# Row part of the position bias: one product for both heads of a pair; the residual read in the middle of the attention

## The reference, cut to what matters

```python
x = x + _L0_conv_ref(_gn(x), ...)     # neighbourhood attention, 7 x 7, 16 registers
x = x + _L1_conv_ref(_gn(x), ...)     # full attention with a position bias
```

```python
q = q * scale
attn = jnp.einsum('bqd,bkd->bqk', q, k)
rel_h = jnp.einsum('bhwc,hkc->bhwk', r_q, Rh)      # row part: depends on the query and the key's row
rel_w = jnp.einsum('bhwc,wkc->bhwk', r_q, Rw)      # column part
attn = attn + rel_h[..., :, None] + rel_w[..., None, :]
out = softmax(attn) @ v, then proj_w, proj_b
```

## Time and profile before

| | us |
|---|---|
| median of the runs | 3226.82 |
| profiled execution, its own time | 3222.15 |
| its span, first to last instruction | 3220.3 |
| TensorE busy | 2905.4 (90%) |
| VectorE busy | 2476.7 (77%) |
| GpSimd busy | 1902.8 (59%) |
| ScalarE busy | 1861.9 (58%) |
| `front` of layer 2 | about 868 to 1218 |
| `attention_full` | 1218 to about 3112 |

### The profile page before, as it was taken

One profiled execution on the slowest core, in us unless ns is written; L12 is line 12 of the kernel. 1 busy time (PEld: TensorE's weight loads), 2 busy tenths in 40 slices (PEclk: granted clock), 3 DMA queues, 4 the chain that ended last, 5 costly groups with the idle time before them and its releaser, 6 DMA issues. The chain is left out here.

```text
span 3220.3 us, 82906 instructions
## 1 busy us (share of the span) xinstructions
PE 2905.4 (90%) x34200; PEld 1874.4 (58%) x34200; DVE 2476.7 (77%) x5171; ACT 1861.9 (58%) x3434; POOL 1902.8 (59%) x1561
## 2 busy tenths in 40 slices
PE   4996999997579885999999999999999999999977
PEld 2453677774335442666666666666666666666644
DVE  6754888885666534888888888888888888888854
ACT  3333676664344432666666666666666666666655
POOL 3452555552110123777777777777777777777762
PEclk9896999998789986999999999999999999999989
DMA  3326555555437658322222222222222233332115
GB/s 142 155 89 147 135 135 141 142 140 192 143 108 215 195 131 203 63 51 52 51 52 52 51 51 51 51 52 52 51 51 51 52 61 59 58 59 54 21 42 147
DMA packets 219836, 301.91 MB, mean 94 GB/s; under 512 B 134394, under 2 KB 172884, under 8 KB 213972
## 3 DMA queue, kind: packets, MB, share of 16 engines
q1 hardware_dynamic: 219460, 296.62, 37.7%
HBM read 196.56 MB, written 92.64 MB: 90 GB/s over the span
## 5 line engine op out<-in xcount | busy, mean ns | idle before, releaser
L1746 POOL TENSOR_TENSOR fprob_low<-fprob 128x768 f16<-128x768 f32 x1008 | 1449.2, 1468 | 445.2 <-ACT fprob L1714 445.2
L1757 DVE TENSOR_REDUCE fpart_max<-fmax_acc 128x1 f32<-128x384 f32 x2592 | 1354.0, 556 | 252.0 <-PE fmax_acc L1585 235.9
L1714 ACT ACTIVATE fprob<-fscores 128x768 f32<-128x768 f32 x1296 | 1049.3, 810 | 592.5 <-PE fscores L1614 592.4
L1585 PE MATMUL fmax_acc<-fk_m,fq_m 128*128 128x384 f16 x2592 | 847.8, 327 | 32.6 <-DMA fident<-in_ident 27.6
L1612 PE MATMUL fscores<-fq_a,fk_a 128*128 128x384 f16 x2592 | 843.0, 325 | 10.6 <-DMA fk_m<-in_one_m 10.6
L1614 PE MATMUL fscores<-fq_b,fk_b 97*128 97x384 f16 x2592 | 846.9, 327 | 0.0
L1638 PE MATMUL fout_acc<-fv,fprob 128*128 128x65 f16 x7776 | 609.4, 191 | 2.5 <-POOL fprob_low L1746 2.1
L1639 PE MATMUL fout_acc<-fv,fprob_low 128*128 128x33 f16 x7776 | 593.8, 179 | 0.0
L1638 PEld LDWEIGHTS fout_acc<-fv,fprob 128*128 128x128 bf16 x7776 | 541.6, 97 | 76.5 <-POOL fprob_low L1746 5.2
L1639 PEld LDWEIGHTS fout_acc<-fv,fprob_low 128*128 128x128 f16 x7776 | 485.6, 96 | 72.5
L1131 POOL TENSOR_TENSOR prob_low<-prob 128x242 f16<-128x242 f32 (+2 forms) x360 | 250.0, 717 | 254.7 <-ACT prob L1089 252.9
(11 more groups left out here) (134 smaller groups left out, 3980.5 us busy)
## 6 DMA issues: line engine op xcount, KB each, us to landing
q_a<-q_hi SPq DMA_DIRECT2D x48, 432.0 KB, 5.7
fq_a<-q_hi SPq DMA_DIRECT2D x48, 432.0 KB, 7.6
q_a<-q_lo SPq DMA_DIRECT2D x24, 432.0 KB, 7.5
row_bias<-bias_slot SPq DMA_DIRECT2D x24, 432.0 KB, 6.8
col_bias<-bias_slot SPq DMA_DIRECT2D x72, 144.0 KB, 4.7
fq_a<-q_lo SPq DMA_DIRECT2D x24, 432.0 KB, 8.6
fq_a<-col_bias SPq DMA_DIRECT2D x24, 432.0 KB, 16.8
fq_b<-row_bias SPq DMA_DIRECT2D x24, 432.0 KB, 5.8
```

The source lines that it names most:

```text
L1585: nc.tensor.matmul(max_acc[:, piece_bank(g, u, j), 0:PIECE], q_m[:, b, tile * 128:(tile + 1) * 128], k_m[:, b, piece * PIECE:(piece + 1) * ...
L1714: nc.scalar.activation(prob[:, k % RING, :].rearrange("p (j n) -> p j n", j=2), scores[:, 2 * (k % 2):2 * (k % 2) + 2, 0:UNIT], ACT.Exp).t ...
L1746: engine.tensor_tensor(prob_low[:, k % RING, :], prob[:, k % RING, :], prob[:, k % RING, :].bitcast(BF16)[:, 1::2], ALU.subtract).then_inc ...
L1757: nc.vector.reduce_max(part_max[:, u % 2, j // PIECES, j % PIECES:j % PIECES + 1], max_acc[:, piece_bank(g, u, j), 0:PIECE], axis=AX.X).th ...
```

## The change

1. In `turn`, for the row axis, one matmul serves both heads of the pair: the same slice of the table with the queries of one image row in 2 heads x 2 images, 192 columns. The two halves of the partitions now hold the upper and the lower half of the image rows: `half` 0 has rows 0 to 23, `half` 1 rows 24 to 47. A group is 4 matmuls. The column axis stays as it is.
2. `banked` and `placed` follow: for the row axis a bank is (head, image) x 96, and `bias_slot` holds (head, image, half of the tokens).
3. `store_item` writes the row part by 8 DMAs (partition half, high or low, head), each 48 partitions of 4608 bytes, which go to DRAM as 96 runs of 2304 bytes. The layout in DRAM is the same.
4. In `attention_full` the residual is read in stages 12, 13 and 14, one DMA each, behind the loads for the next stage and ahead of the store of `heads`.

```diff
-    STORES = (16 * 4, 16 * 4 * NS)
+    STORES = (16 * 8, 16 * 4 * NS)
...
+    HALF = TOK // 2
+    GR = GQ // 2
+
     def banked(g):
 
-        v = side[:, g % 4, 0:B * GQ * SIDE].rearrange("p (b g x) -> p b g x", b=B, g=GQ)
-        return v if g // NG % 2 == 0 else v.rearrange("p b g x -> p b x g")
+        bank = side[:, g % 4, 0:B * GQ * SIDE]
+        if g // NG % 2 == 0:
+            return bank.rearrange("p (i x) -> p i x", i=2 * B)
+        return bank.rearrange("p (b g x) -> p b x g", b=B, g=GQ)
...
+            buf = slot[:, n % 2, lo].rearrange("p (i n) -> p i n", i=2 * B)
+            return buf[:, :, at * GR * SIDE:(at + 1) * GR * SIDE]
...
-                        src = slot[half * 64:half * 64 + SIDE, n % 2, lo].rearrange("p (b n) -> p b n", b=B)
+                        rows = slot[half * 64:half * 64 + SIDE, n % 2, lo]
                         if axis == 0:
-                            sp.dma_start(dram["row_bias"][h, lo * SIDE:(lo + 1) * SIDE], src) \
-                                .then_inc(slot_stored[n % 2], 16)
+                            src = rows.rearrange("p (h b n) -> p h b n", h=2, b=B)
+                            for i in range(2):
+                                dst = dram["row_bias"][2 * pair + i, lo * SIDE:(lo + 1) * SIDE]
+                                sp.dma_start(dst[:, :, half * HALF:(half + 1) * HALF], src[:, i]) \
+                                    .then_inc(slot_stored[n % 2], 16)
                             continue
...
-                for at in range(at0, at0 + GQ):
+                for i in range(GR if axis == 0 else GQ):
                     for half in range(2):
-                        dst = side[half * 64:half * 64 + 64, g % 4, 0:B * GQ * SIDE] \
-                            .rearrange("p (b g x) -> p b g x", b=B, g=GQ)[:, :, at - at0]
-                        src = q[0:3 * D, pair % 2, half].rearrange("p b (r w) -> p b r w", w=SIDE)
-                        src = src[:, :, at, :] if axis == 0 else src[:, :, :, at]
+                        bank = side[half * 64:half * 64 + 64, g % 4, 0:B * GQ * SIDE]
+                        if axis == 0:
+                            at = half * SIDE // 2 + g % NG * GR + i
+                            dst = bank.rearrange("p (i g x) -> p i g x", g=GR, x=SIDE)[:, :, i]
+                            src = q[0:3 * D, pair % 2].rearrange("p h b n -> p (h b) n")[:, :, at * SIDE:(at + 1) * SIDE]
+                        else:
...
-            for t in range(CT):
-                sp.dma_start(x[:, t, 0:ALL], dram["x1"][t * 128:(t + 1) * 128]).then_inc(x_in, 16)
-
             def stage(h, b):
...
                     load_main(h + b, 1 - b)
+                if n >= STAGES // 2 and n - STAGES // 2 < CT:
+                    t = n - STAGES // 2
+                    sp.dma_start(x[:, t, 0:ALL], dram["x1"][t * 128:(t + 1) * 128]).then_inc(x_in, 16)
                 if not is_first(n):
                     store(h - (1 - b), 1 - b)
```

More of the change, by code:

```diff
@@ L295, in store_count @@
         return out
-    STORES = (16 * 4, 16 * 4 * NS)
+    STORES = (16 * 8, 16 * 4 * NS)
     def slot_count(n):
         return sum(STORES[m % 2] for m in range(n % 2, n + 1, 2))
+    HALF = TOK // 2
+    GR = GQ // 2
     def banked(g):
-        v = side[:, g % 4, 0:B * GQ * SIDE].rearrange("p (b g x) -> p b g x", b=B, g=GQ)
-        return v if g // NG % 2 == 0 else v.rearrange("p b g x -> p b x g")
+        bank = side[:, g % 4, 0:B * GQ * SIDE]
+        if g // NG % 2 == 0:
+            return bank.rearrange("p (i x) -> p i x", i=2 * B)
+        return bank.rearrange("p (b g x) -> p b x g", b=B, g=GQ)
     def placed(lo, g):
         n, at = g // NG, g % NG
-        buf = slot[:, n % 2, lo].rearrange("p (b n) -> p b n", b=B)
         if n % 2 == 0:
-            return buf[:, :, at * GQ * SIDE:(at + 1) * GQ * SIDE].rearrange("p b (g x) -> p b g x", g=GQ)
-        return buf.rearrange("p b (x w) -> p b x w", w=SIDE)[:, :, :, at * GQ:(at + 1) * GQ]
+            buf = slot[:, n % 2, lo].rearrange("p (i n) -> p i n", i=2 * B)
+            return buf[:, :, at * GR * SIDE:(at + 1) * GR * SIDE]
+        buf = slot[:, n % 2, lo].rearrange("p (b x w) -> p b x w", b=B, w=SIDE)
+        return buf[:, :, :, at * GQ:(at + 1) * GQ]
     def x_low(queue, engine, i):
@@ L375, in store_item @@
                     for lo in range(2):
-                        src = slot[half * 64:half * 64 + SIDE, n % 2, lo].rearrange("p (b n) -> p b n", b=B)
+                        rows = slot[half * 64:half * 64 + SIDE, n % 2, lo]
                         if axis == 0:
-                            sp.dma_start(dram["row_bias"][h, lo * SIDE:(lo + 1) * SIDE], src) \
-                                .then_inc(slot_stored[n % 2], 16)
+                            src = rows.rearrange("p (h b n) -> p h b n", h=2, b=B)
[3 more added lines that the diff above has]
+                                    .then_inc(slot_stored[n % 2], 16)
                             continue
+                        src = rows.rearrange("p (b n) -> p b n", b=B)
                         for c in range(NS):
@@ L438, in turn @@
                     pe.wait_ge(turn_lo_ready, g - 3)
-                for at in range(at0, at0 + GQ):
+                for i in range(GR if axis == 0 else GQ):
                     for half in range(2):
-                        dst = side[half * 64:half * 64 + 64, g % 4, 0:B * GQ * SIDE] \
-                            .rearrange("p (b g x) -> p b g x", b=B, g=GQ)[:, :, at - at0]
-                        src = q[0:3 * D, pair % 2, half].rearrange("p b (r w) -> p b r w", w=SIDE)
-                        src = src[:, :, at, :] if axis == 0 else src[:, :, :, at]
+                        bank = side[half * 64:half * 64 + 64, g % 4, 0:B * GQ * SIDE]
[4 more added lines that the diff above has]
+                        else:
+                            at = at0 + i
+                            dst = bank.rearrange("p (b g x) -> p b g x", b=B, g=GQ)[:, :, i]
+                            src = q[0:3 * D, pair % 2, half].rearrange("p b (r w) -> p b r w", w=SIDE)[:, :, :, at]
                         last = nc.tensor.matmul(dst, table[0:3 * D, axis, SIDE - 1 - at:SIDE + 63 - at], src,
```

## The result

The changed kernel takes 3231.65 us (median of 20 runs, 3225.61 to 3241.23), the kernel before 3225.59 in the same comparison (20 runs). The ratio is 1.0018, with an interval of 1.0011 to 1.0024: slower by some 5.8 us, where the prediction's step was +3.3. That is inside what was called no change (0.2%), in the range, and on the side that the forecast named. The profiled execution took 3229.65 us, its span 3227.8: 7.5 more than before.

A forecast was written before the change was run, and what follows sets the result against it. TensorE, busy 90% of the span, was taken as the bound, with transfer waits before the attention and at its start. -0.4 + 1.0 + 2.7 = +3.3 us on 3226.82 gave 3230, range 3221 to 3239.

The forecast's parts named there:

- the prediction's step: Whole kernel: -0.4 for the product, +1.0 for the row stores, +2.7 for the residual, sum +3.3 us.
- the side that the forecast named: Whole kernel: slightly slower, by +3.3 us, within the 6.5 us called no change.
- The product, -0.4 us: Layer 2 row-axis bursts: half as many products, same columns streamed, saving 0.01 us a burst, -0.4 us.
- Rival 4: Row-axis product: cheaper by half, -8.3 us, 3222.2 or 3214.9 in all; chance 0.07 together with rival 3.
- The row stores, +1.0 us: Row-item stores: 8 DMAs for 4 cost +0.5 us each at the two places where TensorE waits.
- Rival 2: Row stores: each of eight keeps the price of one of four, +11.6 us, 3240.7 in all; chance 0.13.
- The residual, +2.7 us: Attention start: stage 1's loads move up beside `fk_b`; +1.7 us for its packets, +1.0 behind them.
- The 60 packets: Last 60 rows of `fk_b`, attention start: 123 ns each in place of 95, +1.7 us.
- The upper end is the 128 ns: `fk_b` packets, attention start: at most 128 ns each, +2.0 us and +1.2 behind them.
- The reads in stages 12 to 14, 0 us: Attention stages 12 to 14: residual reads hide in an empty queue, cost 0; some 7 us each if not.
- Rival 1: Attention start: gets shorter as `fk_b` runs undisturbed, -1.6 in place of +2.7, 3225.8 in all; chance 0.18.
- Rival 3: All three terms favourable: products -2.5, stores -2.0, start -1.6, 3220.7 in all; chance 0.07 together with rival 4.

## Why the prediction was right, and what in it was off

**The product, -0.4 us.** Right as far as it can be read. A burst went from 0.46 to 0.45 us, so the halves of the partitions still run together with different weights (else 0.78), and the columns are what is paid (else 0.23). 36 x 0.01 us is the forecast, though 0.01 us is also the last digit that the rows have. Rival 4 falls. What neither the change nor the prediction looked at is the column axis. Its burst has the same 16 products of 96 columns as a row burst; in the kernel before, at full clock:

```profile
966.74 2.08 PE L445 MATMUL side<-bias_q,table 96*64 96x96 f16 x16
968.76 0.34 PE L466 MATMUL acc<-x,w_hi 128*128 128x384 f16 x1
```

2.02 us where the row burst takes 0.46. Apart from the slice of the table, the two differ only in how the queries are read: 48 neighbours for a row, every 48th for a column. No run varied that, so the cause isn't shown; but 36 such bursts are, as an estimate from these rows, 36 x 1.56 = 56 us, far more than all that this change could move.

**The row stores, +1.0 us.** The drain of 12.7 us stayed at the first place and went from 12.5 to 12.8 at the second. The TensorE gaps became 4.08 and 2.46 us where 4.3 and 1.8 were forecast; but they scatter by as much from profile to profile. Their sum is 4.4 to 5.3 us (mean 4.9) in the three profiles with 4 stores, 5.1 to 6.5 (mean 5.5) in the six with 8, and 7.3 in the one with 16: +0.6 us is what 8 stores are worth by the gaps. The half of the change that holds them measures 1.0004 with 1 in its interval; 8 stores of the old layout 0.9996. So between nothing and the 1 us of the forecast. Rival 2 (price by number, +11.6 us) falls: even 16 stores cost 0.14%, some 4.5 us.

**The residual, +2.7 us.** The mechanism was as told: the constants end the wait, `fk_b`'s rows go one behind another, and the loads that move up behind them slow them down. The size was off. The step that failed is "The 60 packets then run beside loads like those of layer 1: 60 x (123 - 95) ns", and with it "The upper end is the 128 ns": the packets took 149 ns each over the whole table, 160 with the move alone, where 123 was taken and 128 the bound (31 rows in the first 4.3 us, 139 ns; 31 in the next 5.0, 161; 35 in the last 5.3, 151). So +4.1 us of pace in place of +1.7, +1.1 behind the table as forecast (+1.0), and a TensorE wait of 16.73 us, +6.2, where some 13 was forecast. Counting only the last 60 rows was no part of the miss: over the whole table, layer 1's pace would have given 97 x (123 - 107) = +1.6 us, the same. It was the pace alone.

Why 123 in layer 1 and 149 here was not found. It doesn't go by bytes: the mean was 305 GB/s at 107 ns, 201 at 149, 190 at 160 and 107 at 90. Nor does it go by the number of packets: layer 1 had 706 in 11.9 us, 59 per us, at 123 ns, and the changed kernel, from 1250 to 1255 us, 258, 52 per us, at 161:

```profile
DMA packets 258, 0.93 MB, mean 186 GB/s; under 512 B 37, under 2 KB 68, under 8 KB 258
```

No run varied stage 1's loads one at a time, so which of them costs the table most stays open.

**The reads in stages 12 to 14, 0 us.** Right. 75.69 and 75.72 us busy of 77.30 with and without one, and the attention from first scores to end is 0.7 us shorter, not longer.

**Sum.** Of the +5.8 us by the runs, +0.6 was forecast for product and stores (measured +1.3, from -1.6 to +4.5) and +2.7 for the residual (measured by itself 0.20%, +6.5 us, from 3.2 to 9.7; by TensorE's wait +6.2). The residual's medians alone say +4.6. The median came to 1.65 us from the forecast in part by luck: the kernel before ran 1.2 us faster in this comparison than in the three runs that the forecast started from. From 3225.59 the same step gives 3228.9, 2.8 below what was measured. Rival 1 (a shorter start) needed the table undisturbed: that is the kernel whose loads are held back, with 90 ns a row on the whole and 73 once nothing else is moved (79 was worked out from the earlier trace rows), and it gained, while the change does the opposite. Rival 3 needed all three terms to be favourable, and none was.

## What to carry to other kernels

Ask of each constant on the path what its row count divides by: here 97 rows went through one engine and 96 + 1 through many, and that one line was worth twice what the change cost, in the other direction. While such a straggler is in flight, taking away a large transfer behind it need not help: here it cost 6 us, through what moved up into its place. And before a product is made cheaper by its count, look at what each burst takes: the bursts that were left alone took four times as long as the ones that were changed. And where a rate under a new load is bounded from rows, the neighbours in those rows must be the neighbours to come: a bound from another stage's loads is only a guess, and the range should say so.

## What the runs showed of the hardware

- One behind another, 97 packets of 1792 bytes took 73 ns each alone (6.6% of 16 engines, one engine's share), 90 on the whole beside other constants, 107 to 108 where most of them went beside the reads of the residual (128 partitions, packets of 18432 bytes; 95 in that part alone), and 149 to 160 beside loads of 32 to 48 partitions; as 96 and 1, all of them took 2.4 us.
- A heavier load by bytes was the milder one: 305 GB/s beside 107 ns, 201 GB/s beside 149 ns.
- Storing 1728 KB from 48 partitions takes 12.7, 12.8 and 12.9 us in 4, 8 and 16 DMAs at the first place, where only the issue grows, 5.8 to 10.2 us, and 12.5, 13.1 and 14.7 at the second.
- Eight products of 192 columns, in two halves of the partitions with different weights, take 0.45 us where 16 of 96 take 0.46. Sixteen of 96 columns whose queries lie 48 elements apart take 2.02 us at the same clock.
